# Scatter sums of a graph layer: 256 pairs of a group and a block in place of 880 of a chunk and a block

## The reference, cut to what matters

```python
xt = x @ W
m = jax.ops.segment_sum(xt[src], dst, num_segments=n) * Binv[:, None]
out = jax.ops.segment_sum(m[dst], src, num_segments=n) * Dinv[:, None]
return out + b
```

## Time and profile before

| | us |
|---|---|
| median of three runs | 5781.98 (5774.1 to 5789.31) |
| span of the profiled execution | 6993.7 |
| TensorE busy in it | 4299.8 |
| POOL busy | 3816.6 |
| VectorE busy | 3576.8 |
| mean granted TensorE clock | 0.797 |

### The profile page before, as it was taken

The page is one execution under the profiler, slowest core; times in us unless marked ns, Lnnn a source line. Parts: engine busy times, 40 slices in busy tenths (PEclk is TensorE's granted clock), DMA queues, the critical chain, the costliest instruction groups (busy, mean ns, idle before and its releaser), DMA issues.

```text
span 6993.7 us, 69182 instructions
## 1 busy us (share of the span) xinstructions
PE 4299.8 (61%) x16858; PEld 2844.9 (41%) x16859; DVE 3576.8 (51%) x11329; ACT 1260.6 (18%) x3299; POOL 3816.6 (55%) x3969
## 2 busy tenths in 40 slices
PE   4778688888785556666645545445344444465995
PEld 1434355555553344444423333333233333344663
DVE  6565566666665444544554444444334443457333
ACT  0356444444441000000010000000000000012331
POOL 2566546666663466666635666665466666610442
PEclk8889899999997778778776777777677766776997
DMA  3300122222223233333323344443433333331114
GB/s 103 110 3 1 41 63 84 84 85 84 84 86 98 71 91 92 93 90 92 90 91 100 115 118 117 118 117 89 132 90 88 90 90 89 90 117 60 63 63 145
DMA packets 322696, 616.76 MB, mean 88 GB/s; under 512 B 79716, under 2 KB 199096, under 8 KB 321848
## 3 DMA queue, kind: packets, MB, share of 16 engines
q0 software_dynamic: 182400, 464.97, 23.1%
q1 hardware_dynamic: 127932, 133.60, 5.8%
q10 hardware_dynamic: 12028, 14.28, 0.6%
HBM read 525.55 MB, written 87.01 MB: 88 GB/s over the span
## 4 chain that ended last, share of the span: by engine, by line
PE 36%; DVE 23%; another core or an unknown queue 20%; issue 16%; DVEq 2%; DMA 1%; SPq 1%; ACT 1%; POOL 0%; ACTq 0%; PEldq 0%; PEld 0%; POOLq 0%
PE PS L1606 15%; DVE rowset L1106 12%; PE PS L1527 10%; PE PS L1788 3%; PE PS L1812 3%; DVE ohg L1115 2%; PE PS L1644 1%; DVE ohg L1110 1%; DVEq L1097 1%; DVE region L1030 1%; PE PS L1805 1%; DMA rowset<-ye_d 1%; DVE region L931 1%; PE PS L1457 1%
## 5 line engine op out<-in xcount | busy, mean ns | idle before, releaser
L596 POOL DMA_INDIRECT rowset<-table,idx x3324 | 3189.3, 959 | 2175.8 <-DVE rowset L1106 1090.5
L1606 PE MATMUL PS<-rowset,ohg 128*128 x7040 | 2235.1, 466 | 2191.5 <-DVE rowset L1106 1371.2
L1106 DVE TENSOR_TENSOR rowset<-rowset,PS 128x257 f32 (+1 forms) x3520 | 1476.3, 419 | 2545.4 <-remote 1617.5
L1606 PEld LDWEIGHTS PS<-rowset,ohg 128*128 128x128 f32 x7040 | 1563.6, 233 | 2819.6 <-issue 2563.0
L1115 DVE TENSOR_SCALAR ohg<-iota,dl 128x128 f32<-128x128 f16 x2640 | 775.9, 295 | 89.3 <-issue 89.3
L1527 PE MATMUL PS<-region 128*128 128x416 f16 x3328 | 703.4, 357 | 0.0
L614 POOL DMA_INDIRECT scattered_d<-rowset x384 | 376.4, 980 | 240.4 <-issue 96.0
L699 ACT ACTIVATE region<-region 128x128 f16<-128x128 f16 x832 | 334.0, 401 | 756.5 <-DVE region L1030 520.5
L1527 PEld LDWEIGHTS PS<-region 128*128 128x128 f16 x3328 | 341.1, 102 | 293.4 <-issue 56.5
L1527 PE MATMUL PS<-rowset,region 128*128 128x416 f16 x1792 | 364.7, 361 | 70.5 <-issue 66.7
L1029 DVE TENSOR_SCALAR region<-iota_c,region 128x832 f16<-128x832 f16 x832 | 383.4, 461 | 24.6 <-issue 24.4
(11 more groups left out here) (322 smaller groups left out, 3377.0 us busy)
## 6 DMA issues: line engine op xcount, KB each, us to landing
rowset<-table,idx POOLq DMA_INDIRECT x3324
table<-rowset SPq DMA_DIRECT2D x21, 896.0 KB, 5.3
region<-xt_d SPq DMA_DIRECT2D x98, 128.0 KB
rowset<-ye_d SPq DMA_DIRECT2D x12, 1024.0 KB, 7.5
xpad_d<-rowset SPq DMA_DIRECT2D x1, 6272.0 KB, 20.6
xn_d<-rowset SPq DMA_DIRECT2D x49, 128.0 KB
xt_d<-rowset SPq DMA_DIRECT2D x49, 128.0 KB
table<-rowset SPq DMA_DIRECT2D x49, 128.0 KB
```

The lines of the kernel that those rows point to most:

```text
L596: gp.indirect_dma_start(rowset[:, at + c % ring, 0:F], None, tables[p], bass.IndirectOffsetOnAxis(idx[p % 2][:, c:c + 1], 0)).then_inc(s_g ...
L1106: TT(a, a, chunk_sum(p, k), ALU.add).then_inc(s_acc[p], 1)
L1606: m = MM(chunk_sum(p, k), ohg[:, k, :], rowset[:, ds(slot_of[k], 1), 0:width(p)].rearrange("p a f -> p (a f)"), start=True, stop=True)
```

## The change

Four chunks make a group, and a pair is now one of a group and a block: 208 + 48 = 256 pairs a pass. Each has four one-hots (one instruction for four in pass 0, four otherwise) and four products that add up in one PSUM bank, and one add. There are 4, 5, 6 and 6 banks for these sums in the four passes. One-hots are made 5 pairs ahead (24 matrices in place of 16). POOL reads from a fourth row of `blk_row` the last pair in which each group takes part, 16 numbers at a time, and waits once a group for just that pair; the rings have 14 and 16 groups. SP does nothing in the passes but count landings; ScalarE's queue issues the loads and stores that SP issued. The side work follows the pairs: the sort takes 4 columns a pair over the first 208, k and v one block every 4 pairs, with a signal on the matmul in place of a drain. From pair 213 on VectorE finishes seven blocks every seven pairs, and ScalarE's queue stores each part as the next table while the pass goes on; only the last part waits for pair 255. The sums of the next pass are cleared by ScalarE behind that.

```diff
     NC = -(-CH // U) * U
     HC = NC // 2
-    PAIR = -(-(CH + NB - 1) // U) * U
-    HP = PAIR // 2
-    NW = -(-PAIR // P)
-    TURNS, SORT_TURNS = PAIR // U, EC // U
+    AG = 4
+    NAG = -(-CH // AG)
+    PAIR = NAG + NB - 1
+    NW = PAIR // P
+    SORT_TURNS = EC // U
...
+    SUMS_FROM = (4, 3, 2, 2)
+
     def banked(p):
-        return 4 if p < 2 else 8
-
-    def group(p):
-        return 2 if p < 2 else 4
-
-    RINGS = (58, 64)
+        return 8 - SUMS_FROM[p]
+
+    RAW = 24
+    OHL = RAW // AG - 1
+    BODY = 4
+    LAST_GROUP = NAG - 1
+    RINGS = (56, 64)
     RING_AT = (NB, 0)
     BEHIND = NB - 1
-    AG = 4
-    NAG = -(-CH // AG)
     AS = 8
     SPAN = P + BEHIND
...
+        def pair_sum(p, v):
+            return PS[:, SUMS_FROM[p] + v % banked(p), 0:width(p)]
...
-            for i in range(NAG // (U // AG)):
-                if i < NB:
-                    sp.wait_ge(s_kv, i + 1)
-                    sp.dma_start(mx["xt"], xt_d[i * P:(i + 1) * P, :].rearrange("p (k n) -> p k n", k=KT)).then_inc(s_xtl, 16)
-                arrivals(1, i * (U // AG))
-            store_table(1)
...
+            arrivals(1, 0, NAG)
+            arrivals(2, 0, NAG)
+            for n in range(2):
+                sp.wait_ge(s_st[n], (NB + 1 - n) // 2 * 32)
...
+            def pairs_through(p, j):
+
+                return nc.values_load_multi_w_load_instructions(
+                    blk_row[p % 2][3:4, j:j + U], engines=(mybir.EngineType.Pool,), min_val=1, max_val=PAIR,
+                    skip_runtime_bounds_check_because="computed on the chip as one more than the number of a pair")[1]
+
+            at_least = pool.alloc_register("at_least")
+
             def gather_pass(p):
                 pool.wait_ge(s_idx, p % 2 + 1)
+                pool.wait_ge(s_bwr, 32)
                 ring, at = RINGS[p % 2], RING_AT[p % 2]
-                for c in range(CH):
-                    if c % AG == 0 and c >= AG * AS:
-                        pool.wait_ge(s_arr[p], c // AG - AS + 1)
-                    if c >= ring:
-                        pool.wait_ge(s_acc[p], U + (c - ring + BEHIND + 1))
-                    gp.indirect_dma_start(rowset[:, at + c % ring, 0:F], None, tables[p],
-                                          bass.IndirectOffsetOnAxis(idx[p % 2][:, c:c + 1], 0)).then_inc(s_g[c // AG % AS], 16)
+                for g in range(NAG):
+                    old = g - ring // AG
+                    if old >= 0 and old % U == 0:
+                        through = pairs_through(p, old)
+                    if g >= AS:
+                        pool.wait_ge(s_arr[p], g - AS + 1)
+                    if old >= 0:
+                        pool.reg_alu(at_least, pool.to_reg(through[old % U]), 1, ALU.max)
+                        pool.wait_ge(s_acc[p], at_least)
+                        settle(pool)
+                    for c in range(g * AG, g * AG + group_size(g)):
+                        gp.indirect_dma_start(rowset[:, at + c % ring, 0:F], None, tables[p],
+                                              bass.IndirectOffsetOnAxis(idx[p % 2][:, c:c + 1], 0)).then_inc(s_g[g % AS], 16)
...
+            def store_part(p, n):
+                act.wait_ge(s_fin, p * NR7 + n + 1)
+                act.dma_start(rows(tables[p + 1], n * R7, R7), accs[p % 2][:, n * R7:(n + 1) * R7, 0:F]).then_inc(s_tab, 16)
+
+            def end_pass(p, part=None):
+
+                for n in range(NR7):
+                    if n == NR7 - 1:
+                        act.wait_ge(s_acc[p], PAIR)
+                        clear(p + 1, 0).then_inc(s_zero, 1)
+                    if part is not None:
+                        part(n)
+                    store_part(p, n)
+                for n in range(1, NR7):
+                    clear(p + 1, n).then_inc(s_zero, 1)
+
+            end_pass(0)
...
-            def add_chunk(p, i, k, block_of):
-                if k % group(p) == 0:
-                    dve.wait_ge(s_mm[p], i * (U // group(p)) + (k // group(p) + 1))
-                dve.wait_ge(s_acc[p], i * U + (U + k))
-                a = accs[p % 2][:, ds(block_of[k], 1), 0:width(p)].rearrange("p a f -> p (a f)")
-                TT(a, a, chunk_sum(p, k), ALU.add).then_inc(s_acc[p], 1)
-
...
+            def one_hots(p, v):
+                at = v * AG % RAW
+                if p == 0:
+                    TT(ohg[:, at:at + AG, :], iota_1[:, :].unsqueeze(1).broadcast_to([P, AG, P]),
+                       dl[0][:, :, v:v + 1].broadcast_to([P, AG, P]), ALU.is_equal).then_inc(s_ohg[p], 1)
+                else:
+                    for j in range(AG):
+                        m = TS(ohg[:, at + j, :], iota_1[:, :], dl[p % 2][:, j, v:v + 1], None, ALU.is_equal)
                     m.then_inc(s_ohg[p], 1)
...
+            def acc_pass(p, body, after=None):
+
+                if p:
+                    dve.wait_ge(s_ohg[p - 1], PAIR)
+                for v in range(OHL):
+                    one_hots(p, v)
+                for v in range(PAIR):
+                    if v % U == 0:
+                        block_of = block_numbers(p, v // U)
+                    body(v)
+                    if v + OHL < PAIR:
+                        one_hots(p, v + OHL)
+                    if p and v % R7 == 0 and v < NB:
+                        dve.wait_ge(s_zero, 2 + (p - 1) * NR7 + v // R7 + 1)
+                    dve.wait_ge(s_mm[p], v + 1)
+                    if v:
+                        dve.wait_ge(s_acc[p], v)
+                    a = accs[p % 2][:, ds(block_of[v % U], 1), 0:width(p)].rearrange("p a f -> p (a f)")
+                    TT(a, a, pair_sum(p, v), ALU.add).then_inc(s_acc[p], 1)
+                    if after is not None and v >= LAST_GROUP + R7 - 1:
+                        n, k = (v - LAST_GROUP - R7 + 1) // R7, (v - LAST_GROUP - R7 + 1) % R7
+                        after(n, k, v)
...
+            def mean(p, n, k, v):
+
+                if k == 0:
+                    dve.wait_ge(s_acc[p], v + 1)
                     if p == 0:
...
+            def sort_body(v):
+                if v <= LAST_GROUP:
+                    for c in range(v * AG, v * AG + AG):
+                        next_column(c // U, c % U)
+                if v == LAST_GROUP + 2:
                     unpack(1)
-                if (i, k) == (SORT_TURNS, 12):
+                if v == LAST_GROUP + 4:
                     stairs(1)
-                if (i, k) == (SORT_TURNS + 1, 12):
+                if v == LAST_GROUP + 11:
                     lanes(1)
 
             dve.wait_ge(s_ones, 1)
-            acc_pass(0, 0, SORT_TURNS, next_column)
-            acc_pass(0, SORT_TURNS, TURNS, next_lanes)
+            acc_pass(0, sort_body, lambda n, k, v: mean(0, n, k, v))
...
+            def biased(n, k, v):
+                if k == 0:
+                    dve.wait_ge(s_acc[1], v + 1)
+                    inverse(1, n)
+                    for b in range(n * R7, (n + 1) * R7):
+                        m = STT(out=accs[1][:, b, 0:F], in0=accs[1][:, b, 0:F], scalar=inv[:, 1, b:b + 1], in1=vecs[:, 0, :],
+                                op0=ALU.mult, op1=ALU.add)
+                    m.then_inc(s_hz, 1)
+                if k == 1 or n == NR7 - 1:
+                    leaky(n)
...
+            def product_pass(p, body):
+                for v in range(PAIR):
+                    if v % U == 0:
+                        slot_of, arrived = slots_of(p, v // U), groups_of(p, v // U)
+                    pe.wait_ge(s_ohg[p], v + 1)
+                    pe.reg_alu(at_least, pe.to_reg(arrived[v % U]), 1, ALU.max)
+                    pe.wait_ge(s_arr[p], at_least)
+                    if v >= banked(p):
+                        pe.wait_ge(s_acc[p], v + 1 - banked(p))
+                    for j in range(AG):
+                        m = MM(pair_sum(p, v), ohg[:, v * AG % RAW + j, :],
+                               rowset[:, ds(slot_of[v % U] + j, 1), 0:width(p)].rearrange("p a f -> p (a f)"),
+                               start=j == 0, stop=j == AG - 1)
+                    m.then_inc(s_mm[p], 1)
+                    body(v)
...
+            def sort_body(v):
+                if v <= LAST_GROUP:
+                    for c in range(v * AG, v * AG + AG):
+                        sort_column(1, c // U, c % U)
+                if v == LAST_GROUP:
+                    close_sort(1)
...
+            def kv_body(v):
+                i = v // BODY
+                if v % BODY == 0 and i < NB:
+                    pe.wait_ge(s_xtl[i % 2], i // 2 * 16 + 16)
+                    pe.wait_ge(s_kn, i + 1)
+                    for h in range(2):
+                        for kt in range(KT):
+                            m = MM(PS[:, h, :], xt_of[i % 2][:, kt, :], mx["wkv"][:, kt, h * INNER:(h + 1) * INNER],
+                                   start=kt == 0, stop=kt == KT - 1)
+                    m.then_inc(s_kv, 1)
+                    dots()
```

More of the change, by code:

```diff
@@ L115, in gps_layer @@
     G = 4
-    FOLD = 16
+    FOLD = 80
```

(31 more changed lines are left out.)

471 lines of the change are left out of this document (181 added, 290 removed).

## The result

| | before | after |
|---|---|---|
| median of the runs, us | 5782.9 | 5743.9 |
| span of the profiled execution | 6993.7 | 5748.2 |
| TensorE busy | 4299.8 | 4273.7 |
| POOL busy | 3816.6 | 3862.9 |
| VectorE busy | 3576.8 | 2847.3 |

The changed kernel is faster by 0.65% (ratio 0.9935, 0.9921 to 0.9949), some 38 us. I had predicted 5792, no change that can be told. The time lies in the range, but the sum had 10 us more, where some 38 fewer were measured.

A forecast was written before the change was run, and what follows sets the result against it. The prediction took POOL's gathers, one per 1.25 us, to bound both kernels. Against 5782 us, turnovers −60, pass 0 +55 and POOL's queue +15 gave +10: 5792 us, no change that can be told; range 5480 to 5880.

The forecast's parts named there:

- turnovers: Between passes, last add to next gather: 89 us shrink to 30, as only the seventh part is left; −60 us.
- pass 0: First pass, with the sort: POOL's 1044 us before, 1095 after, held behind TensorE's sort; taken as +55 us.
- passes 1 to 3: VectorE's and TensorE's changed work lies beside POOL's gathers, against 1039 us a pass; 0.
- POOL's register loads: POOL's queue gains 50 register loads in four passes, taken at 0.3 us each: +15 us.
- both ends: Stages ahead of and behind the passes, 805 and 782 us in the first profile; mostly cancelling between the kernels.
- Rival B: Faster: timed gathers under 1.25 us and real hand-off waits, mostly removed; about 5600 us, range 5340 to 5750; chance 0.30.
- D: Rival taking the first trace at its word, waits real and everything stretched alike: 4935 us; chance 0.04.
- some 6000: Expected sign in the profile after: the span shrinks far more than the time, to some 6000 us.
- C: Slower rival: TensorE's four sort columns a pair hold up pass 0, clock of 0.90 for it; 5882 us; chance 0.16.
- POOL's last 26 groups: End of a pass: scaling and ScalarE stores of the six earlier parts lie beside these gathers and cost nothing.
- gathers × 1.25: Ledger over four passes: 3324 gathers at 1.25 us need at least 4155 us; without POOL's waits the span is 5742.

The follow-up runs named there:

- e0: The kernel before, unchanged, profiled a second time: 5782.9 us, with a span of 5781.1 us.
- e7: The changed kernel with POOL's register loads four times as often, 144 loads more: 5744.8 us (ratio 0.9934).
- e6: The changed kernel with one TensorE product more for each pair of pass 0: 5830.6 us (ratio 1.0082).
- e8: The changed kernel with one TensorE product more for each pair of passes 1 to 3: 5748.2 us (ratio 0.9933).
- e2: The changed kernel, but VectorE scales all seven parts only after the last add: 5798.3 us (ratio 1.003).
- e1: The changed kernel, but pass 0 makes a pair's four one-hots by four tensor_scalar instructions, not one tensor_tensor: 5737.4 us (ratio 0.9926).
- e4: The changed kernel with pass 0's sort spread over 232 pairs and its one-hots made by single tensor_scalar instructions: 5688.0 us (ratio 0.9835).
- e9: The changed kernel, but passes 1 to 3 also make a pair's four one-hots by one tensor_tensor: 5819.2 us (ratio 1.0056).

## Why the prediction was wrong

Spans of e0 and of the changed kernel, part by part (their difference is 32.9 us, that of the medians 39.0; the profiled execution of the changed kernel took 5749.95 us, the slowest of its four, which is the 6 between):

| step | predicted | measured |
|---|---|---|
| turnovers, last add to next gather | −60 | 89.2 to 27.3: −61.9 |
| last gather to last add before them | none | −9.7, of it 15.7 to 7.0 in pass 1 |
| pass 0, first gather to last | +55 (worked out: 1044 to 1095, with the end) | +16.3 (1095.3 to 1111.6) |
| passes 1 to 3, likewise | 0 | +13.7, +6.9, +2.3 |
| POOL's register loads | +15 | 0 (e7) |
| both ends | 0 | −0.5 |
| sum | +10 | −32.9 |

**Right:** that POOL's gathers set passes 1 to 3 of both kernels and TensorE pass 0 of the changed one, and that the first profile's waits weren't the kernel's own (e0, e6, e8). The turnovers, to 2 us; e2 shows that they are the gain. TensorE's part of pass 0: the sort was to take 957 us and took 945, from 670.2 to 1615.4, with 103 gathers left where I had 104; an added product a pair costs 91 us (94 expected in e6), and spreading the sort gives 40 back. Rival B is dead, since there were no hand-off waits to remove and a gather still starts every 1.25 us, and so is D. That the span would shrink to some 6000 was wrong: the stretching was that one execution's, and the span after is 5748.2. C's mechanism is real, but at the granted clock of 0.97 and not 0.90 it costs no more than the forecast had.

**Wrong, the step that failed:** *Pass 0*, in its first half. It set before at "831 × 1.25 + 5 = 1044", with 30 us at most for gathers that something slows, spread over the whole kernel. Measured are 1095.3 from first gather to last, and 1102.3 to the last add. POOL never waits in it; its gathers take 56 us longer in all (842.5 us, where 831 × 0.946 are 786). The earlier trace rows had shown most of this, 829.13 us of POOL in pass 0 against 786 to 788 in the others, and I read past it: all the slow gathers were in the one pass that the term is about. So the kernel before had a good part of that loss already, and the sort's early end added 16 and not 55. e1 shows why the two don't add: the longer gathers lie in time in which POOL would wait for TensorE.

The term's other half, 1095 for the changed kernel up to the last add, came out at 1118.4: 21 us ahead of the sort's first matmul, which I had not charged, 945 for the sort, 145 for the gathers left in place of 130, and 7 at the end. That it is close owes something to the clock: I had worked it out at full clock, and 0.97 was granted, not the 0.90 of the first profile.

**The terms that were mis-sized:** POOL's register loads, charged 15 and hidden (e7); and the scaling and the stores "beside POOL's last 26 groups", which were to cost nothing. In passes 1 and 2 POOL's busy time is 13.6 and 7.0 us higher than in e0, and 18 of those 21 us lie in gathers that run beside the instructions which scale and finish the parts (L1173, L1230, L1237); the longest gather of the kernel takes 2.55 us. These three errors are −39, −15 and +23 us; with the 10 before the last add that I had not charged, and 2 of the turnovers, they make the 43 between +10 and −33.

## What to carry to other kernels

Before anything is argued from waits, lay the span beside the timed runs; if it is far longer, look for the one rate that, taken alone, explains the time (here gathers × 1.25), ask stage by stage whether that rate holds, and have a second profile made before believing the waits of the first. Two limits that lie close together in one stage hide each other: that POOL hardly waits doesn't show that TensorE has slack; adding work to TensorE (e6 against e8) or taking some away (e4 against e1) does. Where an engine's own DMAs set the time, finish and store the results of a stage while it still runs, but with instructions that don't lengthen those DMAs.

## What I had not expected of the hardware

One VectorE instruction can make a POOL gather more than twice as long (at most 2.55 us for 0.95). In pass 0 of the changed kernel (timeline of POOL, then of VectorE, same stretch):

```profile
1643.97 0.94 POOL L586 DMA_INDIRECT rowset<-table,idx  x1 [0.30 <-issue]
1645.22 1.98 POOL L586 DMA_INDIRECT rowset<-table,idx  x1 [0.31 <-issue]
1647.50 1.46 POOL L586 DMA_INDIRECT rowset<-table,idx  x1 [0.30 <-issue]
```

```profile
1645.15 1.22 DVE L1091 SCALAR_TENSOR_TENSOR dl<-iota_c,region 128x1024 f16<-128x1024 f16 x1
1646.51 0.69 DVE L1127 TENSOR_TENSOR ohg<-iota,dl 128x512 f32<-128x512 f16 x1
1647.12 0.42 DVE L1152 TENSOR_TENSOR rowset<-rowset,PS 128x257 f32 x1
1647.45 0.68 DVE L1127 TENSOR_TENSOR ohg<-iota,dl 128x512 f32<-128x512 f16 x1
```

The gather of 1645.22 takes 1.98 us beside an instruction of 1.22 and the start of the next. Each of the 21 gathers over 1.5 us in the changed kernel runs beside an instruction that reads two inputs from SBUF (L1091, L1127, L1173 or L1230). The tensor_scalar of the one-hots, with 0.30 us and one wide input, adds under 3 us to the 309 gathers of pass 2 beside which nothing but it and the adds run, and the sort's comparisons, tensor_scalar instructions of 0.49 and 0.26 us, add 2 us to 155 gathers of pass 0. No run changes an instruction's inputs and leaves its length as it is, so that the inputs are the reason is likely and not shown. The Trainium skill, "SBUF: State Buffer", section "Who interferes with whom", says that a tensor_tensor with both inputs in SBUF contends with GpSimd's reads, and infers that DMAs aren't held up by it, since writing descriptors needs the other interface. The first is in keeping with e9; for the second the measurement decides: indirect DMAs issued by POOL took 74.5 us longer there. Which access of the gather is held isn't shown.

And a granted clock that rises with TensorE's load: with e8's added products it went from 0.88, 0.83 and 0.82 to 0.94, 0.88 and 0.88 in passes 1 to 3, each a mean over a pass of the two levels, 1.2 and 2.4 GHz.
